# Shared-expert chunks split two, three and three around two expert batches, and chunk 6 scored in the last front step

## The chip, the cores and the metric

The kernel runs on one core of one Trainium2 chip. The metric is the device time of one execution in microseconds; before the change it is 677.71 us, the median of three runs (675.24 to 678.16).

## What is computed

Two layers on 4 x 1024 tokens of width 128, all in float32. The first is a convolution plus a scan over the tokens plus a gated MLP, with a layer norm behind it. The second, which the change is about, is a mixture of experts with one shared expert, again with a layer norm behind it. Cut to what matters:

```python
x = layernorm(x + first_layer(x))
scores = sigmoid(x @ gate_w.T)                    # 64 experts in 8 groups
# 4 groups by the sum of their two best, then 8 experts of these, by scores + bias
rw[t, e] = 2.5 * scores[t, e] / sum of the 8 chosen scores (0 where not chosen)
mlp(x, gw, uw, dw) = silu(x @ gw.T) * (x @ uw.T) @ dw.T      # inner width 88
routed = sum over e of rw[:, e] * mlp(x, Wg[e], Wu[e], Wd[e])
shared = mlp(x, Sg, Su, Sd)                       # inner width 2 x 88
x = layernorm(x + routed + shared)
```

## The kernel before

The 4096 tokens are 32 tiles of 128, and 8 chunks of four tiles. Every engine runs its own list of instructions, in the order in which the program writes them; semaphores (`s_...` counted by ACT and DVE, `p_...` by PE, `d_...` by DMAs) tie the lists together. The program has these stages:

- **Front.** A step k from 0 to 8 runs the first layer on chunk k (begin) and k - 1 (MLP), and routes chunk c = k - 2: PE transposes the normed rows (`transpose_x1`) and multiplies by the gate (`logits`, into PSUM tile MI), ACT takes the sigmoid (`scores`, with one table load before and one behind), DVE picks experts in the pieces `group_sums`, `group_seconds`, `compare_groups`, `mask_groups`, `choose`, PE counts places (`ranks`), DVE makes them slots (`take_ranks`). Chunks 0 to 5 are scored inside the front; chunk 6 and the last, chunk 7, are not.
- **Scatter.** POOL writes the rows of tiles 0 to 27 to memory sorted by expert, one indirect DMA for each tile and each of its 8 choices: 224 of them (L487), in the order of the tiles. Tiles 0 to 13 are batch 0, tiles 14 to 27 batch 1. Chunk 7 is not scattered; all experts are run on it, in the dense stage.
- **Shared phase ahead.** PE, ACT and DVE run the shared expert on chunks 0 to 3 (`SH_A = 4`). A chunk is two halves j: `shared_block` (PE, into GU), `shared_silu` (ACT), `shared_hidden` (DVE), then `shared_down` (PE) and `add_shared` (DVE). The results of ACT and DVE lie in `ssil` and `hs`, which are rows of `ol`, the buffer from which the experts' output is later stored. Between these pieces lie the scoring of chunks 6 and 7 and the last placing (`ranks`, `starts`, `tile_experts`, `weight_columns`).
- **Batches.** Each is 44 quads of four 128-row blocks, each block of one expert: SP loads it (L418), PE transposes it (`tr_x`, L780), multiplies (`gate_up`, L791), transposes back (`tr_h`, L800) and multiplies (`down`, L811); ACT takes a copy, a silu and the output, and stores it (L1068); DVE multiplies (`mul_h`) and copies (`take_h`). SP may load a batch when all its scatters have landed. DVE also works out the weights of the slots (`slot_weights`), norms them once (`normalize_weights`, in batch 1), and adds gathered rows.
- **Gather.** POOL fetches the outputs back in the order of the tokens, 224 indirect DMAs (L492) in eight sets of up to four tiles, sets 0 to 3 of batch 0, sets 4 to 7 of batch 1. The gathers of a batch wait until all its stores have landed (`d_st`). They fill two buffers by turns, `gbuf`, halves 0 and 1. DVE adds a set in 8 rounds (`add_round`, L1525): sets 0 and 1 among the quads 60 to 67 and 76 to 83, set 2 from quad 84 on, the others later.
- **Shared phase behind** on chunks 4 to 7. ACT waits for all stores ahead of its first silu, since `ssil` and `hs` lie in `ol`.
- **Dense.** 44 pieces j: PE multiplies chunk 7 by all experts (L851, L852), ACT silu, DVE two products, PE adds up (L860). The third part of its weights is loaded into `ol` (L441) when the shared phase is over. DVE adds sets 4 to 7 between the pieces. Norms and stores of the result follow chunk by chunk.

Two waits set the order around the change: in the shared phase a chunk's `shared_hidden` waits for the `shared_down` of the chunk before, since there is one `hs`:

```python
if c:
    dve.wait_ge(p_sd, c)
v.tensor_tensor(hs[0:I, j, :], GU[0:I, 2 * j + 1, :], ssil[0:I, j, :], ALU.mult).then_inc(s_sh, 1)
```

and POOL starts the gathers of a batch so:

```python
if ts[0] == TFIRST[b]:
    pool.wait_ge(s_gslot, 2 * b + 1)
    for r in range(4):
        pool.wait_ge(d_st[r], 4 * Q0[b + 1])
```

Of the kernel before, what the change touches and what calls it, by code (L numbers as in the profile page):

```python
# [37 lines left out]
P = 128  # L38
# [31 lines left out]
ROUTED = NS - 1  # L70
# [7 lines left out]
SH_A = 4  # L78
# [28 lines left out]
SUM_AT = {0: 60, 1: 76}  # L107
# [22 lines left out]
def build(nc, x, vecs, w_gate, w_up, w_down, b_down, gate_wT, gate_bias, wgu, wd, wdf, sgu, sd, out, xs, os):  # L130
    with ExitStack() as ctx:
# [112 lines left out]
        ssil, hs = ol[:, 0:SJ, :], ol[:, SJ:2 * SJ, :]  # L244
        wtab = sb("wtab", [P, K * E])
        trow = wtab[0:1, 0:2 * max(ET)].rearrange("p (a b) -> p a b", a=2)
# [116 lines left out]

        def ring(c):

            return slice(c % 4 * CT, (c % 4 + 1) * CT)
# [4 lines left out]
        def _(sp):  # L371
# [68 lines left out]
            sp.wait_ge(p_sd, NC)  # L440
# [11 lines left out]
        def _(pool):  # L452
# [43 lines left out]
            for g_, ts in enumerate(SETS):  # L496
                b = batch_of(ts[0])
                if ts[0] == TFIRST[b]:
                    pool.wait_ge(s_gslot, 2 * b + 1)
                    for r in range(4):  # L500
                        pool.wait_ge(d_st[r], 4 * Q0[b + 1])
                for k in range(K):
                    if g_ >= 2:

                        pool.wait_ge(s_acc, ROWS0[g_ - 2] + len(SETS[g_ - 2]) * (k + 1))
                    if k >= 2:
                        pool.wait_ge(d_gat[g_ % 2][k - 2], landed(g_))
                    elif g_:
                        pool.wait_ge(d_gat[(g_ - 1) % 2][K - 2 + k], landed(g_ - 1))
                    for t in ts:  # L510
                        gather(g_, t, k).then_inc(d_gat[g_ % 2][k], 16)

        @block.tensor
        def _(pe):
# [93 lines left out]
            def logits(c):  # L608
                pe.wait_ge(s_x1T, c + 1)
                if c > ROUTED:  # L610
# [115 lines left out]
            def shared_down(c):  # L726
                pe.wait_ge(s_sh, SJ * (c + 1))
                if c == 0:
                    pe.wait_ge(s_x1T, NC)
                elif c == 1:  # L730
                    pe.wait_ge(s_v, NC)
                else:
                    pe.wait_ge(s_res, c - 1)
                if c >= SH_A:
                    pe.wait_ge(s_xg, NQ)
                    pe.wait_ge(s_eo, NQ)
# [149 lines left out]
        def _(act):  # L886
# [211 lines left out]
            def shared_silu(c, j):  # L1098
# [3 lines left out]
                f(ssil[0:I, j, :], GU[0:I, 2 * j, :], ACT.Silu).then_inc(s_ssil, 1)  # L1102
# [6 lines left out]
            for c in range(SH_A):  # L1109
# [4 lines left out]
                if c in (0, 2):  # L1114
                    nc.scalar.preload_act_table(ACT.Sigmoid)
                    scores(6 + c // 2)
                    nc.scalar.preload_act_table(ACT.Silu)

            first_quads(0)
            last_quads(0)  # L1120
            first_quads(1)
# [51 lines left out]
        def _(dve):  # L1173
# [268 lines left out]
            for c in range(SH_A):  # L1442
                shared_hidden(c, 0)
                shared_hidden(c, 1)
                if c:
                    add_shared(c - 1)
                if c == 0:
                    group_sums(6)
                    group_seconds()
                if c == 1:  # L1450
                    compare_groups()
                    mask_groups()
                    choose(6)
                if c == 2:
                    take_ranks(6)
                    count_tiles(NBAT - 1)
                if c == 3:
                    place_tiles(NBAT - 1)
            add_shared(SH_A - 1)
# [42 lines left out]
            def normalize_weights():  # L1502

                w = wk[:, 0:NST * K].rearrange("p (t k) -> p t k", k=K)
                v.tensor_reduce(wsum[:, 0, 0:NST], w, AX_X, ALU.add)
                then(v.tensor_reduce(wsum[:, 0, NST:NT], rw[:, NST:NT, :], AX_X, ALU.add))
                then(v.tensor_scalar(wsum[:, 0, :], wsum[:, 0, :], 1e-20, None, ALU.add))
                then(v.reciprocal(wsum[:, 1, :], wsum[:, 0, :]))
                then(v.tensor_scalar(wsum[:, 1, :], wsum[:, 1, :], ROUTED_SCALE, None, ALU.mult))
                then(v.tensor_tensor(w, w, bc(wsum[:, 1, 0:NST].unsqueeze(2), P, NST, K), ALU.mult))  # L1510
# [40 lines left out]
            def normalize(which):  # L1551
# [53 lines left out]
            weighed(0, 4 * UN, Q0[1] - UN)  # L1605
            for q in range(Q0[1] - UN, Q0[1]):
                quad(0, q, q)
                if q % 2:
                    slot_weights(q // 2, 3 * (q // 2))

            mul_h(Q0[1], 0)
            weighed(1, Q0[1], 2 * NST)
            normalize_weights()
            plain(1, 2 * NST, SUM_AT[0])
            adding(1, 0)
            plain(1, SUM_AT[0] + K, SUM_AT[1])
            adding(1, 1)
            plain(1, SUM_AT[1] + K, NQ - UN)
            for q in range(NQ - UN, NQ):
                quad(1, q, q)  # L1620
                add_round(2, q - (NQ - UN))

            for c in range(SH_A, NC):
# [4 lines left out]
                if c < SH_A + 2:  # L1628
                    add_round(2, UN + 2 * (c - SH_A))
                    add_round(2, UN + 2 * (c - SH_A) + 1)  # L1630
                else:
                    for k in range(UN):
                        add_round(3, UN * (c - SH_A - 2) + k)
# [31 lines left out]
            normalize(tiles(NS))  # L1665
# [37 lines left out]
```

## Time and profile before

| what | us |
|---|---|
| median of three runs | 677.71 |
| the profiled execution, as timed | 671.72 |
| its span, first to last instruction | 670.0 |
| PE busy | 591.1 (88%) |
| DVE busy | 456.4 (68%) |
| POOL busy | 448.0 (67%) |
| ACT busy | 322.1 (48%) |

PE is TensorE, DVE VectorE, ACT ScalarE, POOL GpSimd, SP the engine that issues loads; PEld are PE's weight loads and SPq is SP's queue of DMA issues. A line of the profile names an instruction by the kernel's line (L780 is line 780 above). The stages lie one behind the other: front to about 190 us, shared phase ahead to 222, batch 0 to 358, batch 1 from 363 to 502, shared phase behind to 537, dense to 656, end at 670. POOL scatters from 56.56 to 352.75 us and gathers from 364.63 on, beside all of these. A busy share over the whole span says little here, because each stage has its own limit; the stage has to be found in which an engine is waited for.

### The profile page before, as it was taken

Reading aid. Unit: us, or ns where it says so; the run is one execution under the profiler, and the core shown is the slowest. Engines: PE = TensorE matmul, PEld = TensorE weight load, DVE = VectorE, ACT = ScalarE, POOL = GpSimd, SP = SyncE. Lnnn points to the kernel's source line nnn. Section 1 sums busy time; section 2 is a strip of 40 time slices with the busy share of each in tenths; the row PEclk is TensorE's granted clock in tenths of the full one; section 3 lists DMA queues with packets and bytes.
Section 4 is the critical chain, followed back from the end, with each engine's and each line's share of the span. In section 5 each row is a group of like instructions: output and inputs, shape, how many; then the busy total and the mean of one; then the engine's idle time right before and its main releaser. Section 6 shows DMA issues by size and latency. Waiting matters only on the chain.

```text
span 670.0 us, 13374 instructions
## 1 busy us (share of the span) xinstructions
PE 591.1 (88%) x3456; PEld 473.1 (71%) x3457; DVE 456.4 (68%) x1302; ACT 322.1 (48%) x628; POOL 448.0 (67%) x464
## 2 busy tenths in 40 slices
PE   3976988888889899999996998999996799999991
PEld 2646656654556799999995998999982456666660
DVE  3456598869736889777663765654772768977885
ACT  8564876647353355455552444555541115343251
POOL 1004777777777777777772777777765777777772
PEclk9997999988999999999998998999997979999996
DMA  8962666641113478777755787888864232313221
GB/s 229 357 130 67 150 151 157 142 113 50 52 52 112 133 221 239 224 221 225 221 171 154 203 241 195 226 229 235 224 191 132 54 99 68 83 51 84 51 67 51
DMA packets 124589, 101.32 MB, mean 151 GB/s; under 512 B 15318, under 2 KB 114478, under 8 KB 124078
## 3 DMA queue, kind: packets, MB, share of 16 engines
q1 hardware_dynamic: 63750, 48.41, 27.1%
q0 software_dynamic: 14336, 29.39, 15.2%
q10 hardware_dynamic: 46464, 23.07, 12.0%
q8 instruction: 16, 0.26, 0.2%
q14 instruction: 23, 0.19, 0.1%
HBM read 52.58 MB, written 48.23 MB: 150 GB/s over the span
## 4 chain that ended last, share of the span: by engine, by line
PE 43%; POOL 29%; issue 12%; DVE 6%; ACT 4%; DMA 4%; SPq 1%; DVEq 0%; ACTq 0%; POOLq 0%
POOL xs_dram L487 29%; PE GU L791 8%; PE OT L811 6%; PE GU L851 5%; PE GU L852 5%; PE XT L860 4%; PE XT L780 3%; PE HT L800 3%; DMA xs_dram<-x1r,slots 1%; PE OT L593 1%; DVE x_all L1525 1%; PE GU L572 1%; DMA os_dram<-ol 1%; PE GU L722 1%; PE GU L573 1%
## 5 line engine op out<-in xcount | busy, mean ns | idle before, releaser
L487 POOL DMA_INDIRECT xs_dram<-x1r,slots x224 | 227.8, 1017 | 122.0 <-issue 67.5
L492 POOL DMA_INDIRECT arena<-os_dram,gslots x224 | 218.1, 974 | 87.1 <-issue 58.8
L791 PE MATMUL GU<-wgu_sb,arena 128*128 x704 | 122.5, 318 | 0.1
L791 PEld LDWEIGHTS GU<-wgu_sb,arena 128*128 128x128 f32 x704 | 107.4, 194 | 0.8 <-issue 0.5
L1471 DVE TENSOR_TENSOR mlpw_sb<-GU,mlpw_sb 128x352 f32<-128x352 f32 x88 | 46.1, 524 | 80.7 <-ACT mlpw_sb L1053 70.9
L811 PE MATMUL OT<-wd_sb,arena 88*128 x704 | 94.3, 277 | 2.1 <-ACT ol L1063 1.7
L1063 ACT ACTIVATE ol<-OT 128x512 f32<-128x512 f32 x88 | 52.5, 597 | 85.2 <-PE OT L811 84.3
L811 PEld LDWEIGHTS OT<-wd_sb,arena 88*128 88x128 f32 x704 | 85.5, 192 | 4.2 <-issue 3.3
L1525 DVE SCALAR_TENSOR_TENSOR x_all<-arena,wk,x_all 128x128 f32<-128x128 f32 x224 | 64.2, 344 | 3.7 <-DMA arena<-os_dram,gslots 2.0
L1053 ACT ACTIVATE mlpw_sb<-GU 128x352 f32<-128x352 f32 x88 | 40.8, 463 | 49.8 <-PE GU L791 47.9
L1139 ACT ACTIVATE key<-GU 128x512 f32<-128x512 f32 x44 | 26.3, 597 | 75.2 <-PE GU L852 75.2
L1480 DVE COPY arena<-HT 88x512 f32<-88x512 f32 x88 | 59.6, 677 | 1.2 <-PE HT L800 1.2
L1046 ACT ACTIVATE arena<-XT 128x512 f32<-128x512 f32 x88 | 52.2, 594 | 12.9 <-PE XT L780 12.2
L780 PE MATMUL XT<-ident,arena 128*128 128x128 f32 x352 | 54.0, 276 | 5.0 <-DMA arena<-xs_dram 3.9
L800 PE MATMUL HT<-ident,mlpw_sb 128*88 128x128 f32 x352 | 53.1, 274 | 3.6 <-DVE arena L1480 3.5
L851 PE MATMUL GU<-x_all,wgu_sb 128*128 128x512 f32 x88 | 47.4, 621 | 1.9 <-DVE x1r L1438 1.9
L780 PEld LDWEIGHTS XT<-ident,arena 128*128 128x128 f32 x352 | 41.9, 143 | 6.0 <-DMA arena<-xs_dram 4.1
L852 PE MATMUL GU<-x_all,wgu_sb 128*128 128x512 f32 x88 | 46.1, 606 | 0.0
L800 PEld LDWEIGHTS HT<-ident,mlpw_sb 128*88 128x88 f32 x352 | 40.5, 123 | 6.9 <-DVE mlpw_sb L1471 3.8
L1562 DVE TENSOR_TENSOR key<-GU,key 128x512 f32<-128x512 f32 x44 | 30.3, 688 | 20.4 <-PE XT L860 10.3
L572 PE MATMUL GU<-arena,mlpw_sb 128*128 128x512 f32 x64 | 35.6, 639 | 7.9 <-DVE arena L1214 6.0
L851 PEld LDWEIGHTS GU<-x_all,wgu_sb 128*128 128x128 f32 x88 | 28.4, 328 | 18.6 <-issue 12.3
(195 smaller groups left out, 889.0 us busy)
## 6 DMA issues: line engine op xcount, KB each, us to landing
arena<-xs_dram SPq DMA_DIRECT2D x352, 64.0 KB
os_dram<-ol ACTq DMA_DIRECT2D x88, 256.0 KB
xs_dram<-ol SPq DMA_DIRECT2D x16, 512.0 KB, 4.5
wgu_sb<-wgu_dram SPq DMA_DIRECT2D x1, 5632.0 KB
xs_dram<-x1r,slots POOLq DMA_INDIRECT x224
arena<-os_dram,gslots POOLq DMA_INDIRECT x224
wd_sb<-wd_dram SPq DMA_DIRECT2D x1, 2816.0 KB
x_all<-x_dram SPq DMA_DIRECT2D x8, 256.0 KB, 5.5
```

What stands on the lines that cost most here:

```text
L487: g.indirect_dma_start(out=xs[b], out_offset=bass.IndirectOffsetOnAxis(ap=slots[:, t * K + k:t * K + k + 1], axis=0), in_=x1r[:, t, :], in ...
L492: return g.indirect_dma_start(out=gbuf[:, g_ % 2, t - SETS[g_][0], k, :], out_offset=None, in_=os[batch_of(t)], in_offset=bass.IndirectOff ...
L780: ins = tr(XT[:, i * P:(i + 1) * P], xl[:, u % 4, i * P:(i + 1) * P], ident[:, :])
L791: ins = mm(GU[:, 2 * r + i // 2, (i % 2) * 2 * I:(i % 2 + 1) * 2 * I], xg[:, r, i * P:(i + 1) * P], wgu_sb[:, bass.ds(at[i], 2 * I)], star ...
L800: ins = tr(HT[0:I, i * P:(i + 1) * P], eh[:, u % 2, i * I:(i + 1) * I], ident[:, :])
L811: ins = mm(OT[:, i * P:(i + 1) * P], hT[0:I, u % 2, i * P:(i + 1) * P], wd_sb[:, bass.ds(at[i], P)], start=True, stop=True)
L851: mm(GU[:, r, :], wgu_sb[:, j:E * 2 * I:I], x1T(NS), start=True, stop=True)
L852: mm(GU[:, r + 1, :], wgu_sb[:, HI + j:E * 2 * I:I], x1T(NS), start=True, stop=True).then_inc(p_dg, 1)
L1046: f(xg[:, u % 2, :], XT[:, :], ACT.Copy).then_inc(s_xg, 1)
L1063: f(ol[:, u % 4, :], OT[:, :], ACT.Copy).then_inc(s_eo, 1)
L1480: v.tensor_copy(hT[0:I, u % 2, :], HT[0:I, :]).then_inc(s_ht, 1)
L1525: v.scalar_tensor_tensor(out=x_all[:, t, :], in0=gbuf[:, g % 2, i, k, :], scalar=wk[:, t * K + k:t * K + k + 1], in1=x_all[:, t, :], op0=A ...
```

## The change

Chunk 6 is scored in the front's last step (k = 8), as chunks 0 to 5 are in theirs: `ROUTED` goes from 6 to 7. Shared chunks 0 and 1 run ahead of batch 0 (`SH_A = 2`), chunks 2 to 4 between the batches (`SH_B = 5`), chunks 5 to 7 behind batch 1. The intermediate rows of the shared expert get homes of their own: `ol` ahead of batch 0, half 1 of `gbuf` between the batches, `key` behind, and for every odd chunk `hs` lies in `mlpw_sb`, so that `shared_hidden` waits for the `shared_down` of the chunk before the last. ACT no longer waits for the stores ahead of the phase behind, and SP issues the third part of the dense weights when the stores have landed instead of behind the shared phase. POOL waits for `p_sd` to reach 5 ahead of the gathers of set 1. `normalize_weights` is cut in three: tiles 0 to 13 at quad 36 of batch 0, tiles 14 to 27 at quad 56, the dense part at quad 58. Set 1 is added from quad 68 on and set 2 in quads 80 to 87, set 3 in the phase behind.

```diff
-ROUTED = NS - 1
+ROUTED = NS
...
-SH_A = 4
+SH_A, SH_B = 2, 5
...
-SUM_AT = {0: 60, 1: 76}
+SUM_AT = {0: 60, 1: 68, 2: 80}
...
+        def shared_homes(c):
+            if c < SH_A:
+                ssil, hs = ol[:, 0:SJ, :], ol[:, SJ:2 * SJ, :]
+            elif c < SH_B:
+                ssil, hs = gbuf_late[:, 0:SJ, :], gbuf_late[:, SJ:2 * SJ, :]
+            else:
+                ssil, hs = silF, hF
+            return ssil, hs_odd if c % 2 else hs
...
             for r in range(4):
                 sp.wait_ge(d_st[r], 4 * NQ)
-            sp.wait_ge(p_sd, NC)
             sp.dma_start(flat(ol[:, :, :])[:, 0:NJ * P - 2 * half], wdf[:, 2 * half:NJ * P]).then_inc(d_wdf[2], 16)
...
+                if g_ == 1:
+                    pool.wait_ge(p_sd, SH_B)
...
                     if c == 0:
                         transpose_x1(NS, NC + 1)
-                        logits(6)
-                    elif c > lo:
+                    if c == 1:
+                        ranks(NS - 1)
+                    if c > lo:
                         shared_down(c - 1)
-                    if c == 2:
+                    if c == 1:
                         logits(NS)
-                        ranks(6)
-                    if c == 3:
                         starts(NBAT - 1)
...
             last_quads(0)
+            shared_from(SH_A, SH_B)
+            pe.wait_ge(s_res, SH_B)
             first_quads(1)
             transpose_weights()
             last_quads(1)
-            shared_from(SH_A, NC)
+            shared_from(SH_B, NC)
...
             last_quads(1)
-            for r in range(4):
-                act.wait_ge(d_st[r], 4 * NQ)
-            for c in range(SH_A, NC):
+            for c in range(SH_B, NC):
...
                 dve.wait_ge(s_ssil, SJ * c + j + 1)
-                if c:
-                    dve.wait_ge(p_sd, c)
+                if c >= 2:
+                    dve.wait_ge(p_sd, c - 1)
```

PE ahead of batch 0, before: from the downward product of shared chunk 1 (into OT) to the first transpose of batch 0 (`XT<-ident,arena`). Rows that write GU from `sgu_sb` are shared blocks, those that write MI from `gatew_sb` logits, those that write HT ranks and placing.

```order
L741 MATMUL OT<-sd_sb,ol 128x128 x8
L613 MATMUL MI<-gatew_sb,x_all 128x64 x4
...
L639 MATMUL HT<-ones_bf,sel 64x1 x14
L722 MATMUL GU<-x_all,sgu_sb 88x512
...
L741 MATMUL XT<-sd_sb,ol 128x128 x8
L646 MATMUL HT<-upto_bf,ntile_bf 128x64
L648 MATMUL HT<-ident,count 128x64
L650 MATMUL HT<-ntile_bf,upto_bf 64x1
L741 MATMUL OT<-sd_sb,ol 128x128 x8
L656 MATMUL HT<-wk,base_col 1x176
L657 MATMUL HT<-wk,row_col 1x176
L780 MATMUL XT<-ident,arena 128x128 x8
```

The same place after, from the ranks of chunk 6, which now follow the blocks of shared chunk 1 directly:

```order
L735 MATMUL GU<-x_all,sgu_sb 88x512
L636 MATMUL HT<-base_bf,ones_bf 128x256
...
L651 MATMUL HT<-ones_bf,sel 64x1 x14
L754 MATMUL XT<-sd_sb,ol 128x128 x8
L625 MATMUL MI<-gatew_sb,x_all 128x64 x4
L658 MATMUL HT<-upto_bf,ntile_bf 128x64
L660 MATMUL HT<-ident,count 128x64
L662 MATMUL HT<-ntile_bf,upto_bf 64x1
L754 MATMUL OT<-sd_sb,mlpw_sb 128x128 x8
L668 MATMUL HT<-wk,base_col 1x176
L669 MATMUL HT<-wk,row_col 1x176
L792 MATMUL XT<-ident,arena 128x128 x8
```

The blocks and downward products of two shared chunks are gone from here, and one set of logits stands ahead of the front's last ranks instead.

DVE between the batches, after: the last `slot_weights` of batch 0 (`wk<-wtab`), then hidden rows and additions of shared chunks 2, 3 and 4, then the first product of batch 1. Before, the first of these rows is followed by the last directly.

```order
L1508 TENSOR_REDUCE wk<-wtab 128x8
L1448 TENSOR_TENSOR arena<-GU,arena 88x512 x2
L1448 TENSOR_TENSOR mlpw_sb<-GU,arena 88x512 x2
L1454 TENSOR_TENSOR x_all<-XT,x1r 128x512
L1448 TENSOR_TENSOR arena<-GU,arena 88x512 x2
L1454 TENSOR_TENSOR x_all<-OT,x1r 128x512
L1454 TENSOR_TENSOR x_all<-XT,x1r 128x512
L1480 TENSOR_TENSOR mlpw_sb<-GU,mlpw_sb 128x352
```

Two chunks' hidden rows stand ahead of the first addition, because odd and even chunks have separate `hs`.

## Rows read from the trace of the kernel before

**Rows 1.** Timeline, SP's loads of each batch: start us, us, engine, line, operation.

```profile
207.04 18.89 SPq L418 DMA_DIRECT2D arena<-xs_dram  x22
355.13 10.01 SPq L418 DMA_DIRECT2D arena<-xs_dram  x16
```

**Rows 2.** Timeline, PE between the batches: [idle time before <-its releaser].

```profile
357.19 1.15 PE L811 MATMUL OT<-wd_sb,arena 88*128 x8 [0.87 <-ACT ol L1063]
...
363.09 1.11 PE L780 MATMUL XT<-ident,arena 128*128 128x128 f32 x4 [3.90 <-DMA arena<-xs_dram]
```

**Rows 3.** Timeline, POOL: the first gather, the 113th (batch 1's first), the last.

```profile
364.63 0.97 POOL L492 DMA_INDIRECT arena<-os_dram,gslots  x1 [11.88 <-DMA os_dram<-ol]
...
514.30 0.95 POOL L492 DMA_INDIRECT arena<-os_dram,gslots  x1 [0.30 <-issue]
...
657.02 0.94 POOL L492 DMA_INDIRECT arena<-os_dram,gslots  x1 [0.30 <-issue]
```

**Rows 4.** Timeline, from batch 1's last product over the shared phase to dense.

```profile
501.02 1.15 PE L811 MATMUL OT<-wd_sb,arena 88*128 x8 [0.87 <-ACT ol L1063]
...
510.38 1.08 ACT L1102 ACTIVATE ol<-GU 88x512 f32<-88x512 f32 x2 [7.58 <-DMA os_dram<-ol]
...
511.84 1.98 PE L722 MATMUL GU<-x_all,sgu_sb 128*88 128x512 f32 x2 [6.24 <-DVE ol L1432]
...
537.55 2.08 PE L851 MATMUL GU<-x_all,wgu_sb 128*128 128x512 f32 x2 [1.92 <-DVE x1r L1438]
```

**Rows 5.** Timeline, the end: dense's last product and the last round's addition.

```profile
654.61 1.13 PE L860 MATMUL XT<-key,ol 128*128 128x512 f32 x2 [0.72 <-DVE key L1564]
...
659.44 1.14 DVE L1525 SCALAR_TENSOR_TENSOR x_all<-arena,wk,x_all 128x128 f32<-128x128 f32 x4 [1.96 <-DMA arena<-os_dram,gslots]
```

**Rows 6.** Timeline, the front's last step and the shared phase ahead.

```profile
183.54 0.69 ACT L964 ACTIVATE arena<-GU,vec 128x512 f32<-128x512 f32 x1 [2.25 <-PE GU L573]
...
196.95 1.28 DVE L1432 TENSOR_TENSOR ol<-GU,ol 88x512 f32<-88x512 f32 x2 [3.62 <-ACT ol L1102]
...
205.15 0.36 DVE L1285 MAX8 gtop<-group 128x8 f32<-128x8 f32 x4
...
206.35 0.18 DVE L1296 TENSOR_SCALAR group<-group 128x32 f32<-128x32 f32 x1
...
209.25 0.42 DVE L1312 TENSOR_TENSOR rw<-sel,arena 128x256 f32<-128x256 bf16 x1
...
209.44 1.00 PE L613 MATMUL MI<-gatew_sb,x_all 128*128 128x64 f32 x8
...
211.85 0.60 PE L639 MATMUL HT<-ones_bf,sel 128*64 128x1 bf16 x14
...
222.12 0.66 PE L780 MATMUL XT<-ident,arena 128*128 128x128 f32 x4
```

**Rows 7.** The page's groups, ACT's table loads: busy us, mean ns, idle.

```profile
L1025 ACT ACT_TABLE_LOAD x9 | 11.5, 1283 | 0.2
```

**Rows 8.** Timeline, PE on one shared chunk at full clock: blocks, downward product.

```profile
520.34 1.06 PE L722 MATMUL GU<-x_all,sgu_sb 128*88 128x512 f32 x2 [0.94 <-DVE ol L1432]
...
523.81 1.95 PE L741 MATMUL OT<-sd_sb,ol 88*128 88x128 f32 x16
```

**Rows 9.** Timeline, batch 1: three quads' products around `normalize_weights`, and DVE.

```profile
405.24 1.36 PE L791 MATMUL GU<-wgu_sb,arena 128*128 x8
...
415.29 1.36 PE L791 MATMUL GU<-wgu_sb,arena 128*128 x8
...
417.18 0.52 DVE L1471 TENSOR_TENSOR mlpw_sb<-GU,mlpw_sb 128x352 f32<-128x352 f32 x1 [2.02 <-ACT mlpw_sb L1053]
...
418.25 1.36 PE L791 MATMUL GU<-wgu_sb,arena 128*128 x8
```

**Rows 10.** Timeline, POOL: a round of gathers that waited for an earlier round.

```profile
509.30 0.94 POOL L492 DMA_INDIRECT arena<-os_dram,gslots  x1 [3.96 <-DMA arena<-os_dram,gslots]
```

**Rows 11.** Stretches: PE, PEld, DVE, ACT, POOL busy us; granted clock.

```profile
512.00:514.00 2.00, 2.00 (x3) 0.72 (x4) 1.90 (x7) 0.00 (x0) 1.69 (x2) 0.50 0.25 66
```

More of the change, by code:

```diff
@@ L734, in shared_down @@
                 if c >= SH_A:
-                    pe.wait_ge(s_xg, NQ)
-                    pe.wait_ge(s_eo, NQ)
+                    pe.wait_ge(s_xg, NQ if c >= SH_B else Q0[1])
+                    pe.wait_ge(s_eo, NQ if c >= SH_B else Q0[1])
+                hs = shared_homes(c)[1]
                 dst = OT if c % 2 else XT
@@ L1101, in shared_silu @@
                     act.wait_ge(s_sh, SJ * (c - 1) + j + 1)
-                f(ssil[0:I, j, :], GU[0:I, 2 * j, :], ACT.Silu).then_inc(s_ssil, 1)
+                f(shared_homes(c)[0][0:I, j, :], GU[0:I, 2 * j, :], ACT.Silu).then_inc(s_ssil, 1)
             root_v(NS)
@@ L1120, in _ @@
             last_quads(0)
+            for c in range(SH_A, SH_B):
+                for j in range(SJ):
+                    shared_silu(c, j)
             first_quads(1)
@@ L1441, in _ @@
             inverse_v(NS)
[L1442 to L1459, printed above, removed]
+            shared_hidden(0, 0)
+            shared_hidden(0, 1)
+            mask_groups()
+            choose(NS - 1)
+            shared_hidden(1, 0)
+            shared_hidden(1, 1)
+            take_ranks(NS - 1)
+            count_tiles(NBAT - 1)
+            add_shared(0)
+            place_tiles(NBAT - 1)
+            add_shared(1)
             weight_columns(NBAT - 1)
@@ L1500, in slot_weights, with normalize, normalize_slots, normalize_dense @@
                 dve.wait_ge(s_wk, n + 3)
[L1502 to L1510, printed above, removed]
+            def normalize(w, lo, hi):
+                then(v.tensor_reduce(wsum[:, 0, lo:hi], w, AX_X, ALU.add))
+                then(v.tensor_scalar(wsum[:, 0, lo:hi], wsum[:, 0, lo:hi], 1e-20, None, ALU.add))
+                then(v.reciprocal(wsum[:, 1, lo:hi], wsum[:, 0, lo:hi]))
+                then(v.tensor_scalar(wsum[:, 1, lo:hi], wsum[:, 1, lo:hi], ROUTED_SCALE, None, ALU.mult))
+            def normalize_slots(lo, hi):
+                w = wk[:, lo * K:hi * K].rearrange("p (t k) -> p t k", k=K)
+                normalize(w, lo, hi)
+                then(v.tensor_tensor(w, w, bc(wsum[:, 1, lo:hi].unsqueeze(2), P, hi - lo, K), ALU.mult))
+            def normalize_dense():
+                normalize(rw[:, NST:NT, :], NST, NT)
                 v.tensor_tensor(wtab[:, :].rearrange("p (t e h) -> p t e h", t=CT, h=2),
@@ L1549, in inverse_deviation, with normalize_out @@
                                        in1=csd[:, 1, lo:hi], op0=ALU.mult, op1=ALU.mult).then_inc(s_ncmean, 1)
-            def normalize(which):
+            def normalize_out(which):
                 for t in which:
@@ L1604, in _ @@
                     choose(NS)
-            weighed(0, 4 * UN, Q0[1] - UN)
-            for q in range(Q0[1] - UN, Q0[1]):
+            weighed(0, 4 * UN, Q0[1] - 2 * UN)
+            for q in range(Q0[1] - 2 * UN, Q0[1]):
                 quad(0, q, q)
@@ L1609, in _ @@
                     slot_weights(q // 2, 3 * (q // 2))
[L1611 to L1623, printed above, removed]
+                if q == Q0[1] - 2 * UN:
+                    normalize_slots(0, TFIRST[1])
+            for c in range(SH_A, SH_B):
                 shared_hidden(c, 0)
@@ L1627, in _ @@
                     add_shared(c - 1)
[L1628 to L1631, printed above, removed]
+            add_shared(SH_B - 1)
+            mul_h(Q0[1], 0)
+            weighed(1, Q0[1], 2 * NST)
+            for q in range(2 * NST, 2 * NST + UN):
+                quad(1, q, q)
+                if q == 2 * NST:
+                    normalize_slots(TFIRST[1], NST)
+                if q == 2 * NST + 2:
+                    normalize_dense()
+            adding(1, 0)
+            adding(1, 1)
+            plain(1, SUM_AT[1] + K, SUM_AT[2])
+            adding(1, 2)
+            for c in range(SH_B, NC):
+                shared_hidden(c, 0)
+                shared_hidden(c, 1)
+                if c > SH_B:
+                    add_shared(c - 1)
                     for k in range(UN):
-                        add_round(3, UN * (c - SH_A - 2) + k)
+                        add_round(3, UN * (c - SH_B - 1) + k)
             add_shared(NC - 1)
@@ L1664, in _ @@
             inverse_deviation(3)
-            normalize(tiles(NS))
+            normalize_out(tiles(NS))
 def kernel(**inputs):
```

10 lines of the change are left out of this document (6 added, 4 removed).

## The prediction

> **What bounds the kernel now.** I read the chain of waits first, to see which engines the end was traced back to: PE in the largest part, POOL's scatter in the next. Then I read the timeline at each hand-over of a stage, looking at the releaser in brackets, since a stage counts only from what released it.
>
> Three hand-overs matter. SP issues the loads of batch 1 at 355.13 [rows 1], when the last scatter has landed. PE ends batch 0 at 357.19 + 1.15 = 358.34, and stands until 363.09 for loaded rows [rows 2]. So PE's work up to there has only 4.7 us to lose or to win: a faster front alone would make PE wait longer. Batch 1 ends at 501.02 + 1.15 = 502.17, and ACT, with nothing else to do, waits for the stores and starts its first silu at 510.38 [rows 4]: the stores have landed 8 us after the last product. PE stands 6.24 us for it, and the dense stage begins at 537.55. The third is POOL's. It may gather batch 1 from about 510.2, but does so from 514.30 on [rows 3], since it is late with set 3 of batch 0. From there 111 further gathers take until 657.02, 1.286 us each, the last lands for DVE's addition at 659.44 [rows 5], and the program ends at 670.0. PE's dense products end at 654.61 + 1.13 = 655.74 [rows 5]. So two chains end within a few microseconds: dense on PE, gathers on POOL, and POOL's is the later one. Whoever shortens only one gains little.
>
> The sum is made on the span of the profiled execution, 670.0 us (671.72 as timed). The median is 677.71, 6 us more, for which no row accounts; I take the difference of the sum off the median.
>
> **Scoring chunk 6 in the front.** PE gets one set of logits ahead of the front's last ranks, 1.00 us [rows 6], and all behind it moves by that. ACT gets two table loads of 1.28 [rows 7] and a sigmoid of half the columns of a silu of 0.69. It idles 2.25 at that place [rows 6], and PE's logits add 1.00: 3.25 of cover for at most 2.57 + 0.69 = 3.26, so nothing more is lost; without that cover it would be 3.3 on the path. DVE gets the group sums, in its wait for the last downward product, at nothing. The comparison of the groups, 205.15 to 206.35 [rows 6], now stands ahead of the inverse that chunk 7's norm and then the first shared silu wait for, and costs 0 to 1.2; I take 0.9. The hidden rows of shared chunk 0 end at 196.95 + 1.28 = 198.23 before, so at 200.1 after.
>
> **Two shared chunks fewer ahead of batch 0.** DVE then masks and chooses for chunk 6, 206.35 to 209.67 before [rows 6], 3.3: 203.4. The ranks took from the end of the logits, 210.44, to 212.45 [rows 6], 2.0: 205.5. From there to the first transpose of batch 0 at 222.12 lay 9.67: the blocks of a chunk, 520.34 to 523.81 or 3.47 [rows 8], two downward products of 1.95, and 2.3 of placing, addition and hand-over. After, the blocks are gone and chunk 7's logits, 1.00, come in: 7.2. PE would begin batch 0 at 212.7, 9.4 earlier. Is the data there? SP issues from 207.04 as before, since the scatter of tiles 0 to 13 sets that. At batch 1 sixteen issues, four quads, took 10.01 [rows 1], 2.5 for a quad, less than the 2.96 that PE takes (415.29 to 418.25 [rows 9]). The second quad of batch 1 was there 8.0 after the first issue (363.09); by that it comes at 215.0, where PE wants it at about 214.1. I take a loss of 0.4 (0 to 0.9): batch 0 begins 9.0 earlier. The norming of tiles 0 to 13 at quad 36, five small operations of DVE, costs 0.3 there, an estimate: DVE idles 2.02 in a plain quad [rows 9] but also has slot weights here. Batch 0 ends at 358.34 - 8.7 = 349.6.
>
> **Three shared chunks between.** PE's work is 3 x (3.47 + 1.95) = 16.3, with the wait for the downward product of the chunk before gone. PE then waits for the last addition, about 0.9 by the 0.94 and 1.92 that it waited for DVE at such places [rows 4, 8]. What was idle is now filled and overfilled: the first transpose of batch 1 comes at 366.8, its second some 1.4 later, at 368.2, against 363.09. The data has been there for 5 us, so the scatter no longer sets this; the mix on PE does. Back come about 1.4: before, the first products ran after an idle 3.90 at lengths such as 1.11 for a transpose that takes 0.66 [rows 2, 6]. Net 3.7 later. ACT's silus and DVE's products of this phase are queued behind nothing but the last stores' issue and slot weights, and are done in PE's shadow. POOL's new wait for p_sd holds only set 1; it ends near 365, when POOL is still issuing set 0.
>
> **Batch 1.** The norming in one piece cost: from 405.24 to 418.25 three quads took 13.0 [rows 9], where three at 2.96 are 8.9: 4.1. Cut in two it fits about into DVE's idle 2.02 of a quad; I keep 0.6 (0 to 2). The additions of set 2 fall into quads that DVE has time for. Batch 1 ends 3.7 - 3.5 = 0.2 later, at 502.4. Nearly all that the front won is gone by then.
>
> **Behind batch 1.** The stores land at 510.4, perhaps 0.5 earlier, since POOL gathers nothing meanwhile. POOL is no longer late: batch 0's gathers, from 364.63 before [rows 3], can start when the stores have landed, near 355, and are through by 500. Batch 1's gathers start at 509.9 instead of 514.30. The third part of the dense weights, 0.8 MB, is now loaded just then. A round that met stores and a load of 1 MB waited 3.96 [rows 10]; the bounds are 0 and 4.0, and I take 0.4, since a round has 5 us until it is asked for and the load is smaller and alone. The shared phase behind loses a chunk and the wait for stores: dense begins some 17 earlier. That is worth nothing by itself, because the end hangs on POOL. DVE will then be early for gathered rows, by my count of rounds 2 to 3 us at the end of set 5, which stops PE but not POOL. From the first gather of batch 1 to the end nothing is shortened: 670.0 - 514.30.
>
> The sum: 514.30 becomes 510.3, **4.0 earlier**. 677.71 - 4.0 = 673.7.
>
> On the load beside the gathers, the Trainium skill (DMA: Bandwidth & Descriptors, "Issuing engines are not separate DMA queues") says that DMAs interleave on the same 16 DMA engines whichever engine started them, which speaks against this place for the load. By it alone the first rounds pay for the load, and the time is the first rival's, 677.7, where the row's slack gives 673.7. The trace agrees that gathers are held up beside stores and loads: 3.96 once [rows 10].
>
> **The rivals.** First, no change: the first gathers of batch 1 are held up behind the 0.8 MB load by the full 4.0 of the row, or batch 1 ends that much later because a hand-over ahead of it was cut too fine. For it: the row's wait, and that the sum is a difference of large terms (9.0 won, 17.2 put in, 4.7 of idle time filled, 3.5 regained). Against it: the load alone is half of what met the row's round. It gives 677.7.
>
> Second, more gain: a gather is 0.95 busy with 0.30 of issue [rows 3], 1.25, and 111 of them at 1.25 rather than 1.286 save 4.0: 669.7. For it: POOL starts without a backlog. Against it: most of the excess is in gathers that last longer than 0.95 while DVE is busy, and DVE is no less busy.
>
> Third, slower: in the phase between the batches PE's clock falls. After the idle 6.24 the granted clock was 0.50 of full, 1.2 GHz, from 512 to 514 [rows 4, 11], and a pair of matmuls took 1.98 against 1.06 [rows 4, 8]. At that clock a chunk costs 5.4 more. One chunk would eat the gain, and from two on the kernel is measurably slower: all three give 677.7 - 4.0 + 16.2 = 689.9. Against it: here PE comes from batch 0 without standing for more than about 1 us.
>
> **How the numbers follow.** Forecast 673.7, with its own range 671 to 676: 0.58. First rival 0.25, second 0.09, third 0.08. A measurement tells about 0.5%, 3.4 us, from no change, so "faster" is below 674.3. Of the forecast 0.44 lie there and 0.14 in "same"; with the second rival faster is 0.53, with the first same is 0.39, slower is 0.08. Leaving out the third and part of the second, the range is 668.5 to 678.5.
>
> **What would show it.** Batch 0's first transpose near 213, its last product near 350; batch 1's first transpose near 367 with no wait for a DMA; batch 1's last product within 2 us of 502; the 113th gather 7 to 9 us after it; dense over by about 642 while gathers run on to 653. Were the scatter still waited for at 363, PE's front would have gained more than I think; were the last gather not the end's releaser, the reading of the two chains would be wrong. If the 113th gather starts early and the 130th doesn't, it was the load.

## The result and the profile after

The changed kernel takes 668.94 us (median of four runs, 667.80 to 670.40) against 677.62 for the kernel before, beside it: a ratio of 0.988, 95% interval 0.985 to 0.991, or 8.7 us less. The forecast was 673.7, 4.0 us less. The time lies inside the range, at its lower end; the gain is twice the one forecast. Run again later on one chip, ten runs beside thirteen of the kernel before, the gain was 5.6 us (ratio 0.992, 0.988 to 0.995, or 3.4 to 7.8 us), which doesn't exclude the 4.0.

The two profiled executions differ much less than the medians: spans of 670.0 and 668.7, 1.3 us. Both comparisons matter below, because the question of this case turned out to be why they disagree.

From the page of the changed kernel, the granted clock and the chain that ended last:

```profile
span 668.7 us, 13348 instructions
...
PEclk9997999998989999999999899999999899899985
...
PE 57%; POOL 17%; issue 10%; DVE 5%; ACT 4%; DMA 4%; SPq 2%; POOLq 0%; ACTq 0%; DVEq 0%
```

PE now carries the chain through the phase between the batches into batch 1. Its timeline there (start us, us, engine, line, operation, in brackets the idle time before and its releaser), from batch 0's last product to batch 1's second transpose, the answer to [rows 2]:

```profile
348.95 1.77 PE L823 MATMUL OT<-wd_sb,arena 88*128 x8 [0.87 <-ACT ol L1077]
350.51 1.92 PE L734 MATMUL GU<-x_all,sgu_sb 128*88 128x512 f32 x2
...
365.54 1.95 PE L754 MATMUL XT<-sd_sb,arena 88*128 88x128 f32 x16
368.27 0.66 PE L792 MATMUL XT<-ident,arena 128*128 128x128 f32 x4 [0.78 <-DVE x_all L1454]
369.70 1.02 PE L792 MATMUL XT<-ident,arena 128*128 128x128 f32 x4 [0.78 <-ACT arena L1060]
```

No row waits for a DMA: the loads of batch 1, issued at 354.31 where [rows 1] had 355.13, are there long before PE wants them. The 3.90 of [rows 2] is gone; the second transpose, which waited there, comes 6.6 us later than before, at 369.70 instead of 363.09. Ahead of it, batch 0 starts 10.5 earlier than in [rows 6], at 211.60 instead of 222.12:

```profile
206.75 8.16 SPq L429 DMA_DIRECT2D arena<-xs_dram  x14
...
211.60 0.66 PE L792 MATMUL XT<-ident,arena 128*128 128x128 f32 x4
...
215.43 0.66 PE L792 MATMUL XT<-ident,arena 128*128 128x128 f32 x4 [0.25 <-DMA arena<-xs_dram]
...
222.12 0.66 PE L792 MATMUL XT<-ident,arena 128*128 128x128 f32 x4 [1.12 <-DMA arena<-xs_dram]
```

Here PE does wait for loaded rows, 0.25 and 1.12 us.

POOL's timeline (first gather, 112th, 113th, last; compare [rows 3]) and SP's last load of dense weights, which at its place in SP's list waits for batch 1's stores alone:

```profile
355.21 0.97 POOL L502 DMA_INDIRECT arena<-os_dram,gslots  x1 [3.49 <-DMA os_dram<-ol]
...
499.61 0.94 POOL L502 DMA_INDIRECT arena<-os_dram,gslots  x1 [0.31 <-issue]
512.98 0.94 POOL L502 DMA_INDIRECT arena<-os_dram,gslots  x1 [12.42 <-issue]
...
655.55 0.94 POOL L502 DMA_INDIRECT arena<-os_dram,gslots  x1 [0.30 <-issue]
```

```profile
511.99 0.33 SPq L451 DMA_DIRECT2D ol<-wdf_dram  x1
```

This is the new picture. POOL is done with batch 0 at 500 and idles 12.42 (the profile calls it issue, the row of SP shows what it waits for). Before, it came late; now it waits. The end, beside [rows 4, 5]:

```profile
503.21 1.15 PE L823 MATMUL OT<-wd_sb,arena 88*128 x8 [0.87 <-ACT ol L1077]
...
522.39 1.34 PE L863 MATMUL GU<-x_all,wgu_sb 128*128 128x512 f32 x2 [2.37 <-DVE x1r L1454]
...
645.63 1.47 PE L872 MATMUL XT<-key,ol 128*128 128x512 f32 x2 [3.18 <-DVE key L1580]
...
658.13 1.14 DVE L1541 SCALAR_TENSOR_TENSOR x_all<-arena,wk,x_all 128x128 f32<-128x128 f32 x4 [3.34 <-DMA arena<-os_dram,gslots]
```

The dense stage begins 15 us earlier than before and ends 8.6 earlier, and that moves nothing: DVE's last addition waits for gathered rows, and comes 1.3 earlier than in [rows 5]; the last gather starts 1.5 earlier.

### The profile page after: what moved, and what is told of

Same layout as the page of the kernel before. It is cut to its first block, busy times and chain, and to the rows that moved or that the text cites. A ratio compares the mean times of both kernels' runs of the same rounds, so it can differ in the third digit from the quotient of the medians.

```text
span 668.7 us, 13348 instructions
## 1 busy us (share of the span) xinstructions
PE 590.9 (88%) x3456; PEld 472.6 (71%) x3457; DVE 458.5 (69%) x1310; ACT 322.4 (48%) x628; POOL 447.9 (67%) x464
## 4 chain that ended last, share of the span: by engine, by line
PE 57%; POOL 17%; issue 10%; DVE 5%; ACT 4%; DMA 4%; SPq 2%; POOLq 0%; ACTq 0%; DVEq 0%
PE GU L803 16%; POOL xs_dram L497 12%; PE OT L823 12%; PE XT L792 6%; PE HT L812 6%; POOL arena L502 5%; PE GU L863 2%; PE GU L864 2%; DMA arena<-os_dram,gslots 2%; PE XT L872 2%; PE GU L734 2%; PE GU L735 2%; PE OT L605 1%; PE GU L584 1%; SPq L429 1%
```

## The experiments

**The kernel before, profiled again.** The first question was where the usual 677 us lie, when the profiled execution took 671.7. Two more profiles of the unchanged kernel were taken.

> The kernel before, unchanged, for a second profile beside the time of its usual runs (677.6 us; the one profiled took 671.7). Theory A (the 6 us lie in the hand-over between the batches or in POOL's gathers, both of which the change shortens): the profile, if its time is near 677, shows the first transpose of batch 1 later than 363.1 or the 113th gather later than 514.3 by most of the difference. Theory B (they lie in stretches that the change doesn't touch, the front or the scatters): batch 0's start is late by them, at 226 to 228 instead of 222.1, and the rest follows unchanged. Theory C (only chance in the measuring): the profile again takes 671 to 672.

> The kernel before once more, for a third profile. Theory (its time moves with the start of POOL's first gather, 364.6 in the 671.7 us profile and 369.2 in the 677.5 us one): the 113th gather comes 149.6 to 149.8 after the first one, the end 155.5 after the 113th, and the time is their sum, whatever the front took; half clock at the start of batch 0 when the first gather is late. Rival: the times move with the front alone (first scatter at 56.6 or 58.7), and batch 0 lasts 136 in each.

The profiled executions took 677.47 and 680.10; ten runs of the first kernel had a median of 676.38, like the kernel before beside them (676.21). Here is TensorE in the 11 us behind 222, where batch 0 begins: busy us of PE, PEld, DVE, ACT and POOL with counts, then the granted clock. One row each from the execution that the prediction was built on, from the second and from the third:

```profile
222.00:233.00 11.00, 10.01 (x74) 9.21 (x74) 9.05 (x31) 5.18 (x10) 8.56 (x9) 1.00 0.48 139
```

```profile
222.00:233.00 11.00, 10.22 (x45) 8.62 (x44) 7.13 (x30) 2.26 (x4) 8.48 (x9) 0.53 0.34 102
```

```profile
222.00:233.00 11.00, 9.35 (x40) 7.75 (x41) 8.37 (x34) 1.63 (x3) 8.38 (x9) 0.57 0.30 89
```

The clock there was 2.4 GHz in the first and almost throughout 1.2 GHz, called half clock below, in the others. The last product of the shared phase takes 3.07 instead of the 2.05 of the first execution, and POOL hands the delay on. The second execution, PE from the logits on that [rows 6] has at 209.44, and then POOL (first gather, 112th, 113th):

```profile
211.45 1.00 PE L613 MATMUL MI<-gatew_sb,x_all 128*128 128x64 f32 x8
...
221.29 3.07 PE L741 MATMUL OT<-sd_sb,ol 88*128 88x128 f32 x16 [0.95 <-DVE ol L1432]
...
225.56 1.12 PE L780 MATMUL XT<-ident,arena 128*128 128x128 f32 x4
```

```profile
369.17 0.98 POOL L492 DMA_INDIRECT arena<-os_dram,gslots  x1 [15.34 <-DMA os_dram<-ol]
...
517.52 0.95 POOL L492 DMA_INDIRECT arena<-os_dram,gslots  x1 [0.30 <-DMA arena<-os_dram,gslots]
518.77 0.95 POOL L492 DMA_INDIRECT arena<-os_dram,gslots  x1 [0.30 <-issue]
```

Put beside each other (us; each from the timelines of its own execution):

| execution | time | first transpose, batch 0 | first gather | 113th gather | end of span |
|---|---|---|---|---|---|
| before, first | 671.72 | 222.12 | 364.63 | 514.30 | 670.0 |
| before, second | 677.47 | 225.56 | 369.17 | 518.77 | 675.7 |
| before, third | 680.10 | 227.20 | 370.69 | 521.89 | 678.3 |
| after, first | 670.40 | 211.60 | 355.21 | 512.98 | 668.7 |
| after, second | 668.84 | 213.72 | 355.98 | 511.45 | 667.1 |

The half clock at batch 0 is not all of it. The logits stand 2.0 and 3.6 us later in the second and third execution than in the first (211.45 and 213.03 against 209.44), and the first scatter comes 2.1 to 2.2 later in both (58.73 and 58.68 against 56.56), as the rival of the third run has it. Ahead of that scatter, from 40 to 50 us, the granted clock was 1.00 in the first, 0.83 and 0.66 in the others. Batch 0, 136.2 us long in the first from its first transpose to the end of its last product, took 138.5 in the other two, against that rival. In the second its last product ends 5.7 later (364.10 against 358.35): 2.0 from the front, 3.7 from the stretch at half clock.

In the kernel before, the 113th gather follows the first by 149.7, 149.6 and 151.2. POOL comes to it straight from the 112th, so what batch 0 loses is lost at the end. In the changed kernel it follows by 157.8 and 155.5, which is no constant of POOL's but the stores of batch 1. Theory A held for the second, in that 4.5 of its 5.7 us stand at the 113th gather; but batch 0 starts late too, at 225.56, near theory B's 226. Of the third, where 149.6 to 149.8 and 155.5 were expected and 151.2 and 156.4 came, 2.4 us lie behind the first gather.

The 112 gathers of the kernel before are not free of waits. In the first execution POOL stood twice, for 3.24 and for 3.96 us (the second is in [rows 10]). Both waits begin, at 497.22 and 505.34, 3 to 4 us after SP issued a 1 MB load of dense weights:

```profile
493.00 0.34 SPq L434 DMA_DIRECT2D arena<-wdf_dram  x1
502.25 0.34 SPq L437 DMA_DIRECT2D arena<-wdf_dram  x1
```

```profile
500.46 1.14 POOL L492 DMA_INDIRECT arena<-os_dram,gslots  x1 [3.24 <-DVE x_all L1525]
```

The profile names DVE for this one; by the program POOL waits there for an earlier round of gathers too. The second and third execution have two such waits as well, of 3.3 to 4.1 us. Of the two of the changed kernel one has none above 0.7 and the other one of 3.5, POOL being further on by then. So an early start saves POOL more than the start itself: in the first execution of the changed kernel the first gather comes 9.4 earlier than in the first of the kernel before, the 112th 13.4. Whether the loads cause these waits was not tried.

Of 76 timings of the kernel before that ran beside these experiments, 22 have a mean granted clock of 0.959 or more and take 668.7 to 673.3 (median 671.5); the other 54 have less and take 674.1 to 680.4 (median 677.0). So the one profile that stood ahead of the prediction was of the rarer kind. That the half clock sits at batch 0's start in all of the 54 is inferred from two profiles; only the mean is recorded for the rest.

**The gathers alone late.** The test of that reading in the changed kernel: hold POOL's first gather, and nothing else.

```diff
             for g_, ts in enumerate(SETS):
+                if g_ == 0:
+                    pool.wait_ge(p_tx, Q0[1] + 1)
```

> The changed kernel, with POOL's first gather held until the first transpose of batch 1 (368 to 369), so that the gathers alone start as late as in the 677 us execution of the kernel before (369.2), and nothing else starts later. Theory A (in those executions the gathers' backlog is what the end waits for): 112 gathers take 148 to 150 without a pause, the 113th comes at 517.5 to 519.5 instead of 511.5 to 513 although the stores of batch 1 have landed by 512, the end 5 to 6 later, 674 to 676 us, and the last quads and their stores stay where they are. Rival (POOL catches up, or the end hangs on something else that batch 0 moves): 113th gather by 514, under 672 us.

677.49 us (ten runs, 674.18 to 680.00), ratio to before 1.003 (0.999 to 1.006): the whole gain is gone. In its profile, the quickest of the ten, the stores have landed at 509.01 by SP's row, and POOL comes to the 113th gather at 517.06:

```profile
366.49 0.97 POOL L502 DMA_INDIRECT arena<-os_dram,gslots  x1 [16.34 <-PE XT L794]
```

```profile
515.81 0.94 POOL L502 DMA_INDIRECT arena<-os_dram,gslots  x1 [0.30 <-issue]
517.06 0.95 POOL L502 DMA_INDIRECT arena<-os_dram,gslots  x1 [0.30 <-issue]
```

```profile
509.01 0.33 SPq L451 DMA_DIRECT2D ol<-wdf_dram  x1
```

Batch 1's last matmul starts at 500.66, earlier than in the changed kernel (504.09), so nothing but the gathers can have made it late. The cost is 7 to 8.5 by the medians, more than the 5 to 6 expected; the profiled execution ends 3.7 and 5.3 behind the two of the changed kernel.

**Where the chunks stand.** Five kernels differ from the changed one in the numbers ahead, between and behind (2-3-3 is the changed kernel), with the additions of set 3 spread over the chunks behind:

```diff
-SH_A, SH_B = 2, 5
+SH_A, SH_B = 2, 4
```

The other pairs are 2, 6; 4, 4; 3, 4 and 2, 3. With three or four ahead, DVE's products and additions of the further chunks stand in the front behind `place_tiles`.

> The changed kernel with two shared chunks between the batches and four behind. Theory A (TensorE's work between the batches sets when batch 1 starts, and the landing of its stores sets the gathers and so the end): batch 1's first transpose comes one chunk earlier, at 363 instead of 368.3, as the loads of its tiles (issued at 354) then still land in time; last product at 499, 113th gather near 508, the end 4.5 to 5.5 earlier, 664 us. Theory B (the scatter's last rows and the loads already set the start): the transposes wait for DMA until 366 or later, gain under 2 us. Theory C (the dense stage, one chunk later behind the batch, becomes the bound): its last product later than 647 and no gain, 669 us.

> The changed kernel with four shared chunks between the batches and two behind. Theory A (TensorE releases batch 1, and all behind it follows): batch 1's first transpose at 373.7 instead of 368.3, 113th gather near 518.5, the end 5 to 5.5 later, 674 us. Theory B (the end hangs on the gathers' own backlog on POOL): the 113th gather stays near 513 and the time within 1 us of 669. Theory C (the dense stage sets the end): it starts 5 us later by batch 1 and 5 us earlier by the chunk less behind, and the time stays at 669 us.

> The changed kernel with four shared chunks ahead, none between and four behind, as the kernel before has them; chunk 6 scored in the front, the norming cut, the buffers and the earlier sums stay. Theory A (what pays is that batch 0, its stores and so POOL's first gather come earlier): batch 0 starts at 222 to 226, the first gather runs at 365 to 369 again, POOL gathers without a pause until 514 to 518 although batch 1's stores land by 510, and the time is 672 to 676. Rival (the buffers, the cut and the earlier sums are the gain, and the split only moves work): batch 1 starts at 363 as in the 2-2-4 split, the 113th gather comes at 508, 664 to 666.

> The changed kernel with three shared chunks ahead, one between and four behind. Theory A: POOL's first gather comes at 360.5 to 362, its 112 gathers of batch 0 are issued by 505 to 507, about when batch 1's stores (last product near 499.3) land, near 507; 113th gather at 508 to 509.5, 664 to 666 us, at most 1.5 behind the 2-2-4 split. Rival (every microsecond by which batch 0 starts later is paid at the end): 5 later than the 2-2-4 split, 669 us.

> The changed kernel with two shared chunks ahead, one between and five behind. Theory A (behind the 2-2-4 split, scatter and loads are next: issued 2.9 to 3.2 after the last scatter, landed some 5 us later): batch 1's first transpose waits for DMA and comes at 361 to 363.5, at most 1.5 earlier than with two chunks between; 663 to 665 us. Rival B (TensorE waits so long there that the clock falls to half at the start of batch 1): batch 1's first quads stretch by 2 to 4 us, 666 to 668. Rival C (a chunk less between is again 5 us of gain): 659.

To compare on one chip, the changed kernel and the 2-2-4 split ran again beside 2-1-5:

> The changed kernel once more, on the same chip as the two beside it. Theory A (its time hangs on batch 1's start and no longer on the clock at the start of batch 0, so that the runs scatter less than those of the kernel before): median 668 to 670, spread within 5 us, no half clock in the 11 us behind batch 0's start. Rival (its first runs were lucky): 672 or more, a spread of 10 us like the kernel before.

> The 2-2-4 split once more, beside the changed kernel on the same chip. Theory A: 4.5 to 5.5 faster than the changed kernel, 664 us. Rival (its four first runs were lucky, the split of chunks between and behind gains 2 at most): 666 to 668.

| split | median us (runs) | ratio to before | first gather | first transpose, batch 1 | its last matmul | 113th gather |
|---|---|---|---|---|---|---|
| 4-0-4 | 673.89 (10) | 0.999 (0.995 to 1.003) | 364.62 | 358.80, second 363.08 | 497.52 | 516.07 |
| 3-1-4 | 668.43 (10) | 0.994 (0.989 to 0.998) | 361.17 | 366.63 | 502.45 | 511.57 |
| 2-1-5 | 664.25 (4) | 0.985 (0.980 to 0.991) | 356.70 | 362.33 | 497.88 | 507.76 |
| 2-2-4 | 664.17 (4), 663.63 (4) | 0.983, 0.984 | 356.00 | 362.87 | 499.26 | 508.61 |
| 2-3-3 | 668.94 (4), 670.43 (10) | 0.988, 0.992 | 355.21 | 368.27 | 504.09 | 512.98 |
| 2-4-2 | 674.66 (10) | 0.999 (0.996 to 1.001) | 355.12 | 373.25 | 507.62 | 516.46 |

The times of the gathers and of batch 1 are those of one execution of each kernel, for 2-2-4 and 2-3-3 of the first. All other medians are from other chips, where the kernel before had 676.2 to 677.6; on the one of these three it had 676.05. In time and in batch 1's first transpose, 2-2-4 and 2-4-2 came as their theory A had them.

The 4-0-4 split is the telling one. It keeps all of the change but the place of the chunks, and finishes batch 1 at 497.5, some 6.5 earlier than the changed kernel. Yet it is no faster than the kernel before: its first gather is back at 364.62, SP's row has the stores landed at 505.81, and POOL comes 10 us after them:

```profile
505.81 0.33 SPq L451 DMA_DIRECT2D ol<-wdf_dram  x1
```

```profile
514.83 0.94 POOL L502 DMA_INDIRECT arena<-os_dram,gslots  x1 [0.30 <-issue]
516.07 0.94 POOL L502 DMA_INDIRECT arena<-os_dram,gslots  x1 [0.30 <-issue]
```

So what pays is that batch 0 is stored earlier. Once POOL has slack, PE's start of batch 1 sets the end: a chunk more between costs 4.2 to 5.7, a chunk less gains 4.8 (first runs) and 6.8 (one chip). The changed kernel itself repeated at 670.43, within 4.6 us over ten runs, 0.4 above what theory A had. 2-2-4 is better than both kernels, by 12 us against the kernel before. The further step to 2-1-5 gains nothing. There PE has only one chunk between the batches, and the clock is at half over part of it (0.50 from 352 to 356), the pair of matmuls taking 1.91:

```profile
352.30 1.91 PE L734 MATMUL GU<-x_all,sgu_sb 128*88 128x512 f32 x2
...
355.71 1.52 PE L734 MATMUL GU<-x_all,sgu_sb 128*88 128x512 f32 x2
356.84 14.41 SPq L429 DMA_DIRECT2D arena<-xs_dram  x24
...
359.49 2.05 PE L754 MATMUL XT<-sd_sb,arena 88*128 88x128 f32 x16 [1.41 <-DVE arena L1448]
362.33 0.66 PE L792 MATMUL XT<-ident,arena 128*128 128x128 f32 x4 [0.79 <-DVE x_all L1454]
```

I had expected a DMA wait at that transpose. None is there; PE and DVE still set it, though the loads were issued only 5.5 before. And the 1.4 us by which batch 1's last matmul still comes earlier than with 2-2-4 are in part lost, because POOL is late again. The stores have landed at 505.82 by SP's row; POOL, which has stood 3.98 for an earlier round, comes to the 113th gather straight from the 112th, 1.9 later:

```profile
505.82 0.33 SPq L451 DMA_DIRECT2D ol<-wdf_dram  x1
```

```profile
505.26 0.94 POOL L502 DMA_INDIRECT arena<-os_dram,gslots  x1 [3.98 <-DMA arena<-os_dram,gslots]
506.51 0.94 POOL L502 DMA_INDIRECT arena<-os_dram,gslots  x1 [0.30 <-issue]
507.76 1.05 POOL L502 DMA_INDIRECT arena<-os_dram,gslots  x1 [0.30 <-issue]
```

The 3-1-4 split missed its 664 to 666 by 2.4 and came near its rival's 669. The delay went by PE, since POOL still stood 5.32 ahead of the 113th gather. Batch 0 ends 5 later there (last matmul at 356.26, against 351.33), one chunk at half clock takes PE as long as two at full (clock 0.52 from 354 to 361), and batch 1 starts at 366.63. I had left batch 0's end out of that expectation.

**The norming in one piece.** `normalize_slots(0, NST)` and `normalize_dense` together behind quad 56, none at quad 36:

> The changed kernel with the norming of the routing weights in one piece at quad 56, as before the change, instead of tiles 0 to 13 at quad 36 and the rest at quad 56. By the prediction's term the cut regains 3.5 us of the chain in batch 1 and costs 0.3 in batch 0: batch 1's last product 3 us later than 504.4, the end 3 us later, 672 us. Rival: the vector engine's quads behind it have slack enough that TensorE never waits for it: within 1 us of 669.

671.15 us (ten runs), ratio to before 0.994 (0.991 to 0.997); 0.7 to 2.2 above the changed kernel's two medians. In the traces three quads there, counted by DVE's products, take from 412.36 to 422.11, 9.75, where the changed kernel has 411.04 to 419.32, 8.28. So the cut itself is worth about 1.5, half of what was expected. The 4.1 of [rows 9] was more than the norming. In all three executions of the kernel before, one quad there takes 5.4 between transposes instead of 2.96, 2.45 more. The other 1.7 stand in the first execution alone. After the same wait of 2.01 TensorE ran its next products at half clock in the first execution (0.57 from 410 to 414) and at full clock in the second (1.00 from 414 to 418):

```profile
408.60 0.61 PE L800 MATMUL HT<-ident,mlpw_sb 128*88 128x128 f32 x4 [2.01 <-DVE arena L1480]
...
410.95 2.56 PE L791 MATMUL GU<-wgu_sb,arena 128*128 x8
```

```profile
413.65 0.61 PE L800 MATMUL HT<-ident,mlpw_sb 128*88 128x128 f32 x4 [2.01 <-DVE arena L1480]
...
415.70 1.36 PE L791 MATMUL GU<-wgu_sb,arena 128*128 x8
```

The 0.95 between 2.45 and 1.5 may come from the place, behind quad 56 rather than ahead of it; that place alone was not tried.

**Sums and load as before.** The additions of sets 1 and 2 late again, and the third load of dense weights behind the shared products:

```diff
-SUM_AT = {0: 60, 1: 68, 2: 80}
+SUM_AT = {0: 60, 1: 76}
...
+            sp.wait_ge(p_sd, NC)
```

> The changed kernel with two of its moves taken back: the sums of sets 1 and 2 at the quads they had before (76, and the last four quads and the first chunk behind) instead of 68 and 80, and the last load of the dense stage's weights held back until the shared products are done. Theory A (neither is on the path: set 3's and 4's gathers wait for POOL and for the stores, and the dense stage has 9 us to spare): 113th gather within 0.7 of 513, within 1 us of 669. Rival (set 3's gathers or those behind the batch wait for buffers that come free later, or chunks 5 to 7 and the dense stage come late behind the sums): 2 to 5 later, 671 to 674, with waits of POOL on the vector engine's sums, or the dense stage's last product past 651.

670.42 us (ten runs); the changed kernel's ten took 670.43. The 113th gather comes 8.75 after the start of batch 1's last matmul, in the changed kernel 8.89. Together the two moves are worth nothing here that these runs show, and nothing points to a cost of the load beside the gathers; since both were taken back at once, a small gain of one could hide a small cost of the other.

## Why the prediction was right and where it was wrong

**The mechanism.** Three steps came as told. Batch 1 is no longer released by the scatter but by PE's work between the batches, at 368.27 with no DMA wait (forecast 366.8). POOL is through with batch 0 by 500 and waits for the stores. The end hangs on the last gathers, not on the dense stage. The 4-0-4 split and the late gathers show the second by taking it away; the series of splits shows the first by its slope.

**The step that failed** is the sentence that the median lies 6 us above the profiled execution, "for which no row accounts; I take the difference of the sum off the median". The 6 us were not a constant. In the second profile 3.7 us come from TensorE's half clock at the start of batch 0 and 2.0 from the front ahead of it, and the path by which they reached the end was POOL's backlog, just what the change removes. I had used the backlog as a term of 4.1 us, 514.30 less 510.2. In the other two profiles it is larger: counted from the first silu behind the same stores (510.38, 513.96 and 515.30) the 113th gather comes 3.9, 4.8 and 6.6 later. Against the second profile of before, the 113th gather comes 5.8 and 7.3 earlier, and the span ends 7.0 and 8.6 earlier. The eleven profiles of the changed kernel and its variants show full clock in the first 11 us of batch 0; before, one of three does. Each is one execution, though, and the changed kernel's fourteen timed runs differ in mean clock as well, 0.955 to 0.966. In its first profile the last half clock ahead of batch 0 lies between 195 and 203 (0.57 there). Whether half clock stays away from batch 0 in every run, and why, was not settled. A late front alone seems to be taken up by the slack: in the second profile of the changed kernel the logits come 2.1 later than in the first (209.45 against 207.33), and the span ends 1.6 earlier.

The Trainium skill (TensorE: Matmul & The Clock Gate, "What's actually happening") says of the ramp at a kernel's start that the number of matmuls at the low clock varies between runs of one kernel, and puts its penalty at less than 1% of a typical span. Here the variation shows in the middle of the kernel too, 1.00, 0.53 and 0.57 in the same stretch, and the medians of the two groups of runs lie 5.5 us apart, 0.8%. Against a gain of 8.7 that is nearly two thirds.

**The terms on the profiled pair.** There the forecast of 4.0 was too high, since the span moved by 1.3. The 113th gather came at 512.98, not 510.3:

- Batch 0 started 10.5 earlier, not 9.0, but ended at 350.72, not 349.6. The data for its first quads was late (the waits of 0.25 and 1.12 above): its first five quads took 13.63 from transpose to transpose, against 11.67 in the kernel before. I had allowed 0.4 to 0.9 for the loads; it was 2.0. Another 0.6 went to the last product, 1.77 at half clock instead of 1.15. So 7.6 us came off the end of batch 0 in place of 8.7.
- Between the batches 17.55, forecast 17.2.
- From the first transpose to the last product of batch 1 136.1, forecast 135.6. The second transpose took 1.02, half clock; in the second profile of the changed kernel it took 0.63, and that stretch was 1 us shorter.
- The stores landed 7.6 after the last product, forecast 8.0; the first gather followed 1.0 after them. Forecast 7.9 for both, measured 8.6.

These are 1.1, 0.4, 0.5 and 0.7: 2.7 together. The norming's 4.1, of which 3.5 were to be regained, held 1.7 of half clock that only the profiled execution has. So errors of opposite sign met: the profiled pair gave 1.3 in place of 4.0, the usual runs of the kernel before lay 5.9 above its profiled one, and the profiled run of the changed kernel was the slowest of its four, 1.5 above their median. 1.3 + 5.9 + 1.5 make the 8.7. That the time fell inside the range is in part luck.

**The rivals.** "No change", by the load of 0.8 MB beside the first gathers, finds nothing for it in the kernel that puts the load back: its time is the same. "More gain" gave nearly the measured time, but for a reason that is wrong: 111 gathers took 142.57, 1.284 each, where it was 1.286; their pace didn't change. "Slower" came in small: the clock in the phase between was at half only for its first 2 us and just behind it; the stretch 350 to 372 has 0.89. How near it was, 3-1-4 and 2-1-5 show.

## What to carry to other kernels

When the profiled execution is not near the median, find out what the median has more before costing a change on the profile; compare its mean clock with that of the timed runs, and ask which chain would carry such a delay to the end. A change that gives slack to that chain can win part of the run-to-run loss as well: on one chip the runs of the kernel before spread over 6.9 us, those of the changed kernel over 4.6. And when work is taken out of one phase to start a chain earlier, only so much should go into the next phase as the data for it leaves idle: here two chunks between the batches cost no more than one, and the third cost 5 us. Look also at whether the chain that was given slack still has it after the next step: with 2-1-5 it was gone again.

## What was unexpected

The same instructions of the kernel before ran with TensorE at 2.4 or at 1.2 GHz in one stretch of 11 us. Batch 0 started 3.4 us later there, 2.0 of them from the front, and the end came 5.7 later. One shared chunk between the batches took PE 12.0 us from the start of batch 0's last product to batch 1's first transpose (354.61 to 366.63, 3-1-4) and two took 12.4 (350.45 to 362.87, 2-2-4): less work lost by the clock what it saved.
